# Three-sweep graph network on one core: constants in one late transfer, the input by chunks, the first band as two tiles

## The chip, the core and the metric

One core of one Trainium2 chip runs the kernel. The metric is the device time of one execution in microseconds (us), the median of several runs. The profile is one further execution of the same kernel; its "span" runs from its first to its last instruction. Engines: PE is TensorE (PEld its weight loads), DVE is VectorE, ACT is ScalarE, POOL is GpSimd, SP is SyncE, which here only issues DMAs.

## The reference

All arrays are float32. `x` is 4096 x 128, `adj` is 4096 x 4096, all weights are 128 x 128.

```python
def _mlp(x, W1, b1, W2, b2, W3, b3):
    a = jax.nn.leaky_relu
    x = a(x @ W1 + b1, NEG_SLOPE)
    x = a(x @ W2 + b2, NEG_SLOPE)
    return a(x @ W3 + b3, NEG_SLOPE)

u, v = (x, v_node_feats)
for _ in range(3):
    v = _mlp(adj @ u, uv_W1, uv_b1, uv_W2, uv_b2, uv_W3, uv_b3)
    u = _mlp(adj @ v, vu_W1, vu_b1, vu_W2, vu_b2, vu_W3, vu_b3)
y = _layernorm(x + v)
return _layernorm(y + adj @ (y @ gcn_weight))
```

## The kernel before

The work is six products with the same 4096 x 4096 matrix (five through the network, one for the last layer). The output rows are cut into 8 **chunks** of 512. The matrix comes from memory in **bands** of 1 MB, each 128 partitions by 2048 elements: one chunk of rows against one chunk of columns. A band is two **tiles** of 128 x 1024. 500 tiles are loaded in all and the list `visits` names 768 visits, since a tile may serve two sums.

To keep float32 accuracy each tile is split: ACT makes a rounded copy `high` (`split`, L442 to L446), DVE makes the rest `low` = raw - high (L568 to L570), and PE then runs three matmuls for each half of a tile (`multiply`, L777, matmuls of L790): six matmuls of 512 columns a visit. The input `x` is split in the same way, chunk by chunk, by `raise_x` (ACT, L450) and `lower_x` (DVE, L575) ahead of the first eight bands. Four of the seven weights are split by `raise_weights` (ACT, L453 to L457) and `lower_weights` (DVE, L578 to L581).

All engines follow one plan. Each runs a loop over the step n, one step for one visit, and issues what is due in that step; semaphores order the engines. In step n an engine first does what belongs to a chunk of finished sums, then its tiles. A tile's `high` is due about six visits ahead of its own visit, its `low` four ahead. Steps 0 to 15 are the first chunk of rows (bands 0 to 7, one visit for each tile). In step 16 ACT rounds the first finished sum (`raise_sum`, L471 to L473), in step 17 DVE makes its rest (`lower_sum`, L607 to L609), and in step 19 PE runs the first dense layer (`layer_1`, L719): three matmuls, L708 and L709 on the rounded sum and L711 on the rest. Before them it waits until all four weights are split. Before the change ACT and DVE split the weights in step 15 (L531 and L667): on ACT behind the split of tile 20 and ahead of that of tile 21, on DVE ahead of `low` of tile 19.

Buffers: `raw` holds 4 bands (`RAWS` = 8 tiles), `high` and `low` 8 tiles each. SP issues all bands and all of `x` on one hardware queue, in program order; band b (from 4 on) is issued when DVE has lowered both tiles of band b - 4:

```python
                if t >= RAWS:
                    sp.wait_ge(low_ready, t - RAWS + IN_BAND)
```

The input comes in four pieces of 1, 1, 2 and 4 chunks (256, 256, 512 and 1024 KB), so the queue's order before is: x piece 0, band 0, x piece 1, band 1, x piece 2, band 2, band 3, x piece 3, band 4, band 5 and so on. The 13 transfers of weights and biases (four biases of 128 x 1, seven weights and two spread biases of 128 x 128, 0.59 MB) are issued by POOL on the software queue right at the start (L427 to L431); one semaphore counts them all.

Of the kernel before, what the change touches and what calls it, by code (L numbers as in the profile page):

```python
# [12 lines left out]
D = 128  # L13
# [11 lines left out]
RAWS = 8  # L25
# [4 lines left out]
BANKS = 5  # L30
HELD = 8

X_PIECES = [1, 1, 2, 4]

OPENED = 3
SLOPE = 0.01
# [207 lines left out]
            holder[s.bank] = i  # L244

def gnn_kernel(nc, adj, x_nodes, weights, biases, spread, out):
    plan = Plan()
    tiles, visits, sums, chunks = plan.tiles, plan.visits, plan.sums, plan.chunks
    END = len(visits) + 16  # L250
# [1 line left out]
    with ExitStack() as ctx:  # L252
        def sbuf(name, shape, dtype=F32):
            return ctx.enter_context(nc.sbuf_tensor(name, shape, dtype))
# [4 lines left out]
        def sem(name):  # L259
            return ctx.enter_context(nc.semaphore(name))  # L260
# [9 lines left out]
        part = sbuf("part", [D, N - CHUNK])  # L270
        w_high = {name: sbuf(f"w_high_{name}", [D, D], F32R) for name in SPLIT}
        w_low = {name: sbuf(f"w_low_{name}", [D, D], F32R) for name in SPLIT}
        w = {name: sbuf(f"w_{name}", [D, D]) for name in WEIGHTS}
        b = {name: sbuf(f"b_{name}", [D, 1]) for name in BIASES}
        b_spread = {name: sbuf(f"b_{name}", [D, D]) for name in SPREAD}
        eps = sbuf("eps", [D, 1])
        h = [sbuf(f"h{i}", [D, CHUNK]) for i in range(2)]
        h_high = sbuf("h_high", [D, CHUNK], F32R)
# [8 lines left out]
        layer = [psum(f"layer{i}", [D, CHUNK]) for i in range(2)]  # L287
        proj = psum("proj", [D, CHUNK])

        x_loaded = [sem(f"x_loaded{i}") for i in range(len(X_PIECES))]  # L290
        consts_loaded = sem("consts_loaded")
        consts_set = sem("consts_set")
        band_loaded = [sem(f"band_loaded{s}") for s in range(RAWS // IN_BAND)]
# [30 lines left out]
        out_stored = sem("out_stored")  # L324
        last_stored = sem("last_stored")

        N_CONSTS = 16 * (len(WEIGHTS) + len(BIASES) + len(SPREAD))
        FINAL = len(chunks) - CHUNKS
        NORM = FINAL - CHUNKS

# [2 lines left out]

        def raw_of(t):
            return raw[t % RAWS // IN_BAND][:, bass.ds(t % IN_BAND * TILE, TILE)]

        def piece_of(chunk):
            return next(i for i in range(len(X_PIECES)) if chunk < sum(X_PIECES[:i + 1]))

        def block_in(tile, j):  # L340
            return tile[:, j * D:(j + 1) * D]
# [56 lines left out]

        @block.sync
        def _(sp):  # L400
            def load_x(piece):
                of_piece = bass.ds(sum(X_PIECES[:piece]) * CHUNK, X_PIECES[piece] * CHUNK)
                sp.dma_start(resid[:, of_piece], x_nodes[:, of_piece]).then_inc(x_loaded[piece], 16)

            def load(t):
                if t >= RAWS:
                    sp.wait_ge(low_ready, t - RAWS + IN_BAND)
                sp.dma_start(raw[t % RAWS // IN_BAND][:], adj[tiles[t][0], tiles[t][1] // IN_BAND]).then_inc(
                    band_loaded[t % RAWS // IN_BAND], 16)

            for t in range(0, len(tiles), IN_BAND):
                for piece in range(len(X_PIECES)):
                    if t == sum(X_PIECES[:piece]) * IN_BAND:
                        load_x(piece)
                load(t)

            for i in (len(chunks) - 2, len(chunks) - 1):
                sp.wait_ge(normed_ready, i - NORM + 1)
                sp.dma_start(out[sum_of(i).chunk], part_of(sum_of(i).chunk)).then_inc(last_stored, 16)
            sp.wait_ge(last_stored, 32)  # L420

        @block.gpsimd
        def _(pool):
            nc.gpsimd.memset(eps[:], EPS).then_inc(consts_set, 1)
            for name in BIASES:
                pool.dma_start(b[name][:], biases[name]).then_inc(consts_loaded, 16)  # L427
            for name in WEIGHTS:
                pool.dma_start(w[name][:], weights[name]).then_inc(consts_loaded, 16)
            for name in SPREAD:  # L430
                pool.dma_start(b_spread[name][:], spread[name]).then_inc(consts_loaded, 16)  # L431
            for i in range(FINAL, len(chunks) - 2):
                pool.wait_ge(normed_ready, i - NORM + 1)
                pool.dma_start(out[sum_of(i).chunk], part_of(sum_of(i).chunk)).then_inc(
                    first_stored if i == FINAL else out_stored, 16)
            pool.wait_ge(first_stored, 16)
            pool.wait_ge(out_stored, 16 * (CHUNKS - 3))
# [2 lines left out]
        @block.scalar  # L440
        def _(act):
            def split(t):  # L442
                act.wait_ge(band_loaded[t % RAWS // IN_BAND], 16 * (t // RAWS + 1))
                if t >= SLOTS:
                    act.wait_ge(visited, plan.closing[t - SLOTS] + 1)
                nc.scalar.activation(high[t % SLOTS][:], raw_of(t), ACT.Copy).then_inc(high_ready, 1)  # L446

            def raise_x(c):
                act.wait_ge(x_loaded[piece_of(c)], 16)
                nc.scalar.activation(p_high[0][:, blocks_of(c)], resid[:, blocks_of(c)],  # L450
                                     ACT.Copy).then_inc(p_high_ready, 1)

            def raise_weights():  # L453
                act.wait_ge(consts_loaded, N_CONSTS)
                act.wait_ge(consts_set, 1)
                for name in SPLIT:
                    nc.scalar.activation(w_high[name][:], w[name][:], ACT.Copy).then_inc(w_high_ready, 1)  # L457
# [70 lines left out]
                nc.scalar.activation(h[i % 2][:], acc[sum_of(i).bank][:], ACT.Copy).then_inc(taken, 1)  # L528

            for n in range(END):  # L530
                if n == TILES - 1:  # L531
                    raise_weights()
                for i, chunk in enumerate(chunks):
                    if n == chunk.start and not chunk.halves and not finishes(i):
                        take(i)
                    if layered(i):
                        if n == chunk.start and chunk.halves:
                            raise_sum(i)
                        if n == chunk.start + (LAYER_1 if chunk.halves else WHOLE_LAYER_1):
                            first_layer(i)  # L540
                        if n == chunk.start + (LAYER_2 if chunk.halves else WHOLE_LAYER_2):
                            second_layer(i)
                        if n == chunk.third + THIRD:
                            third_layer(i)
                    if normed(i):
                        if n == chunk.third + ROOT:
                            deviation(i)
                        if n == chunk.third + NORMALIZE:
                            normalize(i)
                            raise_normed(i)  # L550
                    if not layered(i):
                        if n == chunk.start + LAST_ROOT:
                            deviation(i)
                        if n == chunk.start + LAST_NORMALIZE:
                            normalize(i)
                for s in sums:
                    if s.goal == "keep" and n == s.read:
                        keep(s)
                for t in range(len(tiles)):
                    if n == split_at[t]:  # L560
                        if t % IN_BAND == 0 and t // IN_BAND < CHUNKS:
                            raise_x(t // IN_BAND)
                        split(t)
# [3 lines left out]
        def _(dve):  # L567
# [96 lines left out]
                                        ALU.subtract).then_inc(p_low_ready, 1)  # L664

            for n in range(END):
                if n == TILES - 1:  # L667
                    lower_weights()
                for i, chunk in enumerate(chunks):
                    if n == chunk.start and finishes(i):  # L670
# [170 lines left out]
```

## Time and profile before

| | |
|---|---|
| runs | 1181.62 us, median of 3 (1181.33 to 1182.02) |
| profiled execution, its own time | 1181.15 us |
| its span, first to last instruction | 1179.2 us |
| PE busy | 1154.8 us, 98% of the span |
| DVE, ACT busy | 739.8 us (63%), 680.8 us (58%) |
| read from memory | 264.8 MB, 226 GB/s over the span |

1.95 us of the profiled execution lie outside its span. The rows below come from this execution. Their times are in us from the first instruction. In a timeline row stand start, length, engine, line, operation, output<-input and shape, with the idle time before it and what ended that in brackets; "x2" means that two neighbours of a kind are merged. In a row of stretches stand the stretch, its length, the busy time of PE, PEld, DVE, ACT and POOL (with counts), the granted TensorE clock, the busy share of the DMA engines and GB/s.

### The profile page before, as it was taken

To read this page: it belongs to the slowest core of one execution; us is meant where nothing else is said; L and a number is where in the kernel's file an instruction comes from. 1 tells how busy PE (TensorE), PEld (TensorE's weight loads), DVE (VectorE), ACT (ScalarE), POOL (GpSimd) and SP (SyncE) were. 2 spreads that over 40 slices of the span, in tenths; PEclk is the share of its full clock that TensorE was granted. 3 is DMA by queue.
4 is the path that set the end of the run, shared out by engine and by line. 5 is a ranking of instruction groups with operands and counts; after the bars stand their busy time and mean duration, and the time that the engine had idled before them with its cause. 6 is when DMAs were issued, how large, how long until landed. Compare 5 with 4: busy or idle time off the path is not lost.

```text
span 1179.2 us, 13786 instructions
## 1 busy us (share of the span) xinstructions
PE 1154.8 (98%) x5216; PEld 950.7 (81%) x5216; DVE 739.8 (63%) x879; ACT 680.8 (58%) x855; POOL 10.5 (1%) x24
## 2 busy tenths in 40 slices
PE   5999999999999999999999999999999999999997
PEld 3788888888788888888888878888887888888886
DVE  5986555554845554765564484555578655669996
ACT  5876544555554444764454474544477655557784
POOL 2000000000000000000000000000000000000000
PEclk9999999999999999999999999999999999999999
DMA  8987665644834446645544574444657454458994
GB/s 351 382 317 276 230 248 214 250 160 189 306 148 186 178 185 219 261 169 193 214 183 162 209 289 176 178 178 178 250 215 266 162 185 181 185 195 342 353 347 173
DMA packets 37823, 267.82 MB, mean 227 GB/s; under 512 B 4464, under 2 KB 4464, under 8 KB 5632
## 3 DMA queue, kind: packets, MB, share of 16 engines
q1 hardware_dynamic: 36864, 264.78, 60.0%
q0 software_dynamic: 896, 2.17, 0.5%
q8 instruction: 43, 0.70, 0.2%
q14 instruction: 20, 0.16, 0.0%
HBM read 264.83 MB, written 2.10 MB: 226 GB/s over the span
## 4 chain that ended last, share of the span: by engine, by line
PE 91%; DVE 5%; DMA 3%; ACT 1%; issue 1%; ACTq 0%; SPq 0%; DVEq 0%
PE acc L790 82%; PE proj L746 3%; DVE low L570 3%; DMA raw<-adj_dram 3%; PE layer L711 1%; PE layer L708 1%; PE layer L709 1%; PE layer L740 1%; PE layer L729 1%; DVE stats L644 0%; ACT part L513 0%; DVE h L640 0%; ACT high L446 0%; DVE h L604 0%; DVE moments L647 0%
## 5 line engine op out<-in xcount | busy, mean ns | idle before, releaser
L790 PE MATMUL acc<-high,p_low 128*128 128x512 f32 x1536 | 609.3, 397 | 14.2 <-DVE low L570 14.2
L570 DVE TENSOR_TENSOR low<-raw,high 128x1024 fp32r<-128x1024 f32 x500 | 584.5, 1218 | 36.8 <-ACT high L446 36.8
L790 PE MATMUL acc<-low,p_high 128*128 128x512 f32 x1536 | 599.6, 390 | 0.0
L790 PE MATMUL acc<-high,p_high 128*128 128x512 f32 x1536 | 598.9, 390 | 0.0
L446 ACT ACTIVATE high<-raw 128x1024 fp32r<-128x1024 f32 x500 | 500.2, 1050 | 80.9 <-DMA raw<-adj_dram 40.8
L790 PEld LDWEIGHTS acc<-high,p_low 128*128 128x128 f32 x1536 | 289.1, 188 | 78.9 <-DVE low L570 17.8
L790 PEld LDWEIGHTS acc<-high,p_high 128*128 128x128 f32 x1536 | 289.1, 188 | 61.4 <-issue 2.9
L790 PEld LDWEIGHTS acc<-low,p_high 128*128 128x128 f32 x1536 | 288.9, 188 | 61.4
L473 ACT ACTIVATE h_high<-h 128x512 fp32r<-128x512 f32 x21 | 13.3, 632 | 134.1 <-DVE h L604 134.1
L604 DVE TENSOR_TENSOR h<-acc,part 128x512 f32<-128x512 f32 x36 | 24.8, 689 | 100.8 <-PE acc L790 93.2
L614 DVE TENSOR_TENSOR h_low<-h,h_high 128x512 fp32r<-128x512 f32 x32 | 22.1, 692 | 70.2 <-ACT h L483 70.2
L619 DVE TENSOR_TENSOR h<-proj,b_uv_b 128x512 f32<-128x512 f32 x24 | 16.6, 690 | 63.9 <-PE proj L746 63.9
L609 DVE TENSOR_TENSOR h_low<-acc,h_high 128x512 fp32r<-128x512 f32 x11 | 7.6, 691 | 77.8 <-ACT h_high L473 77.8
L498 ACT ACTIVATE p_high<-h 128x512 fp32r<-128x512 f32 x32 | 20.2, 632 | 48.5 <-DVE h L619 48.0
L473 ACT ACTIVATE h_high<-acc 128x512 fp32r<-128x512 f32 x11 | 6.6, 596 | 72.1 <-PE acc L790 72.1
L619 DVE TENSOR_TENSOR h<-proj,b_vu_b 128x512 f32<-128x512 f32 x16 | 11.1, 691 | 41.6 <-PE proj L746 41.6
L488 ACT ACTIVATE h<-layer,b_uv_b 128x512 f32<-128x512 f32 x24 | 16.5, 688 | 30.3 <-PE layer L711 24.3
L481 ACT ACTIVATE h_high<-layer,b_uv_b 128x512 fp32r<-128x512 f32 x20 | 13.7, 686 | 34.1 <-PE layer L711 34.1
L500 ACT ACTIVATE h<-h 128x512 f32<-128x512 f32 x40 | 24.8, 620 | 9.9 <-DVE h L619 9.8
L746 PEld LDWEIGHTS proj<-w_uv_W,h 128*128 128x128 f32 x192 | 25.1, 191 | 2.0
L463 ACT ACTIVATE part<-acc 128x512 f32<-128x512 f32 x36 | 21.4, 595 | 7.4 <-PE acc L790 7.0
L746 PE MATMUL proj<-w_uv_W,h 128*128 128x128 f32 x192 | 25.3, 275 | 0.0
(64 smaller groups left out, 379.6 us busy)
## 6 DMA issues: line engine op xcount, KB each, us to landing
raw<-adj_dram SPq DMA_DIRECT2D x250, 1024.0 KB, 4.9
out_dram<-part POOLq DMA_DIRECT2D x6, 256.0 KB, 5.1
resid<-x_dram SPq DMA_DIRECT2D x1, 1024.0 KB, 18.2
resid<-x_dram SPq DMA_DIRECT2D x2, 256.0 KB, 5.9
resid<-x_dram SPq DMA_DIRECT2D x1, 512.0 KB, 13.0
out_dram<-part SPq DMA_DIRECT2D x2, 256.0 KB, 2.0
w_uv_W<-uv_W_dram POOLq DMA_DIRECT2D x3, 64.0 KB, 7.8
w_vu_W<-vu_W_dram POOLq DMA_DIRECT2D x3, 64.0 KB, 7.9
```

The lines of the kernel that those rows point to most:

```text
L446: nc.scalar.activation(high[t % SLOTS][:], raw_of(t), ACT.Copy).then_inc(high_ready, 1)
L463: nc.scalar.activation(part_of(s.chunk), acc[s.bank][:], ACT.Copy).then_inc(part_kept, 1)
L473: nc.scalar.activation(h_high[:], summed(i)[:], ACT.Copy).then_inc(sum_raised, 1)
L488: nc.scalar.activation(h[i % 2][:], layer[1][:], ACT.Prelu, bias=b[f"{way_of(i)}_b2"][:], alpha=SLOPE).then_inc(second_ready, 1)
L498: nc.scalar.activation(p_high[k % 2][:, blocks_of(c)], h[i % 2][:], ACT.Prelu, alpha=SLOPE).then_inc(p_high_ready, 1)
L500: nc.scalar.activation(h[i % 2][:], h[i % 2][:], ACT.Prelu, alpha=SLOPE).then_inc(third_ready, 1)
L570: nc.vector.tensor_tensor(low[t % SLOTS][:], raw_of(t), high[t % SLOTS][:].bitcast(F32), ALU.subtract).then_inc(low_ready, 1)
L604: nc.vector.tensor_tensor(h[i % 2][:], acc[s.bank][:], part_of(s.chunk), ALU.add).then_inc(total_ready, 1)
L614: nc.vector.tensor_tensor(h_low[:], h[i % 2][:], h_high[:].bitcast(F32), ALU.subtract).then_inc(first_lowered, 1)
L619: nc.vector.tensor_tensor(h[i % 2][:].rearrange("p (j d) -> p j d", d=D), proj[:].rearrange("p (j d) -> p j d", d=D), b_spread[f"{way_of(i ...
L746: done = nc.tensor.matmul(block_in(proj, j), block_in(source, j), weight[:], start=True, stop=True)
L790: done = nc.tensor.matmul(bank[:], p[parity][:, at:at + D], a[slot][:, columns], start=(n == s.opens and j == 0 and m == 0), stop=(n == s. ...
```

## The change

- The 13 small transfers on POOL's queue go. One DRAM tensor holds all weights, the two spread biases and the four biases side by side (128 rows of 4624 bytes), and SP loads it in one transfer, issued after band 7 and ahead of band 8. In the chip's memory it is one tile `const`, of which the old names are slices.
- The input comes in eight chunks of 256 KB, each issued right ahead of its band (chunk k ahead of band k, k = 0 to 7), each with its own semaphore.
- Band 0 is loaded as two transfers of one tile each (rows of 4096 bytes instead of 8192), with a semaphore for the first tile.
- The weights are split in step 17 instead of step 15: on ACT behind the split of tile 22 and ahead of that of tile 23; on DVE behind `low` of tile 20, ahead of the rest of the sum and of `low` of tile 21.

The queue's order after: x chunk 0, tile 0, tile 1, x chunk 1, band 1, ..., x chunk 7, band 7, constants, band 8, band 9 and so on.

```diff
-X_PIECES = [1, 1, 2, 4]
+CONSTS_BEHIND = TILES
...
-        w = {name: sbuf(f"w_{name}", [D, D]) for name in WEIGHTS}
-        b = {name: sbuf(f"b_{name}", [D, 1]) for name in BIASES}
-        b_spread = {name: sbuf(f"b_{name}", [D, D]) for name in SPREAD}
+        const = sbuf("const", [D, (len(WEIGHTS) + len(SPREAD)) * D + len(BIASES)])
+        w = {name: const[:, bass.ds(i * D, D)] for i, name in enumerate(WEIGHTS)}
+        b_spread = {name: const[:, bass.ds((len(WEIGHTS) + i) * D, D)] for i, name in enumerate(SPREAD)}
+        b = {name: const[:, bass.ds((len(WEIGHTS) + len(SPREAD)) * D + i, 1)] for i, name in enumerate(BIASES)}
...
-            def load_x(piece):
-                of_piece = bass.ds(sum(X_PIECES[:piece]) * CHUNK, X_PIECES[piece] * CHUNK)
-                sp.dma_start(resid[:, of_piece], x_nodes[:, of_piece]).then_inc(x_loaded[piece], 16)
+            def load_x(c):
+                sp.dma_start(resid[:, blocks_of(c)], x_nodes[:, blocks_of(c)]).then_inc(x_loaded[c], 16)
 
             def load(t):
+                if t == 0:
+                    sp.dma_start(raw_of(0), adj[tiles[0][0], 0, :, 0:TILE]).then_inc(first_loaded, 16)
+                    sp.dma_start(raw_of(1), adj[tiles[0][0], 0, :, TILE:]).then_inc(band_loaded[0], 16)
+                    return
...
             for t in range(0, len(tiles), IN_BAND):
-                for piece in range(len(X_PIECES)):
-                    if t == sum(X_PIECES[:piece]) * IN_BAND:
-                        load_x(piece)
+                if t == CONSTS_BEHIND:
+                    sp.dma_start(const[:], consts).then_inc(consts_loaded, 16)
+                if t // IN_BAND < CHUNKS:
+                    load_x(t // IN_BAND)
                 load(t)
...
             nc.gpsimd.memset(eps[:], EPS).then_inc(consts_set, 1)
-            for name in BIASES:
-                pool.dma_start(b[name][:], biases[name]).then_inc(consts_loaded, 16)
-            for name in WEIGHTS:
-                pool.dma_start(w[name][:], weights[name]).then_inc(consts_loaded, 16)
-            for name in SPREAD:
-                pool.dma_start(b_spread[name][:], spread[name]).then_inc(consts_loaded, 16)
...
             def split(t):
-                act.wait_ge(band_loaded[t % RAWS // IN_BAND], 16 * (t // RAWS + 1))
+                if t == 0:
+                    act.wait_ge(first_loaded, 16)
+                else:
+                    act.wait_ge(band_loaded[t % RAWS // IN_BAND], 16 * (t // RAWS + 1))
...
             def raise_weights():
-                act.wait_ge(consts_loaded, N_CONSTS)
+                act.wait_ge(consts_loaded, 16)
...
             for n in range(END):
-                if n == TILES - 1:
+                if n == TILES + 1:
                     raise_weights()
...
             for n in range(END):
-                if n == TILES - 1:
+                if n == TILES + 1:
                     lower_weights()
```

## Rows read from the trace of the kernel before

**Rows 1.** The page: busy time of PE, and PE in 40 slices of the span.
```profile
PE 1154.8 (98%) x5216; PEld 950.7 (81%) x5216; DVE 739.8 (63%) x879; ACT 680.8 (58%) x855; POOL 10.5 (1%) x24
...
PE   5999999999999999999999999999999999999997
```

**Rows 2.** Stretches of the opening, and the last store of 256 KB (last row).
```profile
2.00:3.50 1.50, 0.00 (x0) 0.00 (x0) 0.00 (x0) 0.02 (x1) 1.50 (x3) 1.00 0.85 201
...
6.00:7.50 1.50, 0.00 (x0) 0.00 (x0) 0.00 (x0) 0.00 (x0) 1.50 (x4) 1.00 0.35 116
...
16.00:26.00 10.00, 8.60 (x36) 6.51 (x36) 7.43 (x8) 5.82 (x8) 0.00 (x0) 1.00 1.02 424
...
1177.65:1178.35 0.70, 0.00 (x0) 0.00 (x0) 0.00 (x0) 0.00 (x0) 0.00 (x0) 0.50 0.96 366
```

**Rows 3.** PE's waits from 0 to 60: us in total, times, longest us.
```profile
PE acc L790 <- DVE low L570: 13.4, 4, 10.0
```

**Rows 4.** Timeline of PE, from its first matmul to the first dense layer.
```profile
9.97 0.79 PE L790 MATMUL acc<-high,p_low 128*128 128x512 f32 x1 [9.97 <-DVE low L570]
...
10.99 0.63 PE L790 MATMUL acc<-low,p_high 128*128 128x512 f32 x1
...
11.42 0.63 PE L790 MATMUL acc<-high,p_low 128*128 128x512 f32 x1
...
27.88 0.50 PE L790 MATMUL acc<-high,p_low 128*128 128x512 f32 x1 [1.57 <-DVE low L570]
...
43.82 0.47 PE L708 MATMUL layer<-h_high,w_low_uv_W 128*128 128x512 f32 x1 [0.22 <-ACT h_high L473]
...
45.51 0.50 PE L711 MATMUL layer<-h_low,w_high_uv_W 128*128 128x512 f32 x1 [0.98 <-DVE h_low L609]
```

**Rows 5.** The chain of waits from 0 to 60: start, us, what.
```profile
34.74 5.63 DMA raw<-adj_dram
...
46.01 4.08 PE acc L790 x18
```

**Rows 6.** Timeline of ACT in the opening.
```profile
4.16 0.63 ACT L450 ACTIVATE p_high<-resid 128x512 fp32r<-128x512 f32 x1 [2.15 <-DMA resid<-x_dram]
7.61 2.00 ACT L446 ACTIVATE high<-raw 128x1024 fp32r<-128x1024 f32 x2 [2.81 <-DMA raw<-adj_dram]
9.98 0.63 ACT L450 ACTIVATE p_high<-resid 128x512 fp32r<-128x512 f32 x1 [0.37 <-DMA resid<-x_dram]
13.54 2.01 ACT L446 ACTIVATE high<-raw 128x1024 fp32r<-128x1024 f32 x2 [2.94 <-DMA raw<-adj_dram]
...
18.05 2.00 ACT L446 ACTIVATE high<-raw 128x1024 fp32r<-128x1024 f32 x2 [1.86 <-DMA raw<-adj_dram]
...
37.91 2.01 ACT L446 ACTIVATE high<-raw 128x1024 fp32r<-128x1024 f32 x2 [0.46 <-DMA raw<-adj_dram]
40.39 1.06 ACT L446 ACTIVATE high<-raw 128x1024 fp32r<-128x1024 f32 x1 [0.47 <-DMA raw<-adj_dram]
41.36 0.49 ACT L457 ACTIVATE w_high_uv_W<-w_uv_W 128x128 fp32r<-128x128 f32 x2
41.75 0.49 ACT L457 ACTIVATE w_high_vu_W<-w_vu_W 128x128 fp32r<-128x128 f32 x2
```

**Rows 7.** Timeline of DVE around the first dense layer.
```profile
42.09 0.48 DVE L581 TENSOR_TENSOR w_low_vu_W<-w_vu_W,w_high_vu_W 128x128 fp32r<-128x128 f32 x2
42.50 2.35 DVE L570 TENSOR_TENSOR low<-raw,high 128x1024 fp32r<-128x1024 f32 x2
44.77 0.68 DVE L609 TENSOR_TENSOR h_low<-acc,h_high 128x512 fp32r<-128x512 f32 x1
```

**Rows 8.** DMA queues from 5.5 to 8: the software queue's packets, MB, share.
```profile
q0 software_dynamic: 52, 0.00, 1.6%
```

**Rows 9.** Two stretches behind PE's last matmul.
```profile
1172.50:1176.50 4.00, 0.00 (x0) 0.00 (x0) 2.16 (x11) 1.67 (x5) 0.00 (x0) 1.00 0.00 0
1176.70:1179.00 2.30, 0.00 (x0) 0.00 (x0) 0.00 (x0) 0.07 (x1) 0.00 (x0) 0.50 0.30 114
```

More of the change, by code:

```diff
@@ L244, in place_banks, with gnn_kernel @@
             holder[s.bank] = i
-def gnn_kernel(nc, adj, x_nodes, weights, biases, spread, out):
+def gnn_kernel(nc, adj, x_nodes, consts, out):
     plan = Plan()
@@ L288, in gnn_kernel @@
         proj = psum("proj", [D, CHUNK])
-        x_loaded = [sem(f"x_loaded{i}") for i in range(len(X_PIECES))]
+        x_loaded = [sem(f"x_loaded{c}") for c in range(CHUNKS)]
+        first_loaded = sem("first_loaded")
         consts_loaded = sem("consts_loaded")
@@ L325, in gnn_kernel @@
         last_stored = sem("last_stored")
-        N_CONSTS = 16 * (len(WEIGHTS) + len(BIASES) + len(SPREAD))
         FINAL = len(chunks) - CHUNKS
@@ L335, in raw_of @@
             return raw[t % RAWS // IN_BAND][:, bass.ds(t % IN_BAND * TILE, TILE)]
-        def piece_of(chunk):
-            return next(i for i in range(len(X_PIECES)) if chunk < sum(X_PIECES[:i + 1]))
         def block_in(tile, j):
@@ L448, in raise_x @@
             def raise_x(c):
-                act.wait_ge(x_loaded[piece_of(c)], 16)
+                act.wait_ge(x_loaded[c], 16)
                 nc.scalar.activation(p_high[0][:, blocks_of(c)], resid[:, blocks_of(c)],
@@ L831 @@
     x_nodes = put("x_dram", _np.asarray(inputs["x"]).reshape(N // D, D, D).transpose(1, 0, 2).reshape(D, N))
-    weights = {k: put(f"{k}_dram", inputs[v]) for k, v in _WEIGHTS.items()}
-    biases = {k: put(f"{k}_dram", _np.asarray(inputs[v]).reshape(D, 1)) for k, v in _BIASES.items()}
-    spread = {k: put(f"{k}_dram", _np.broadcast_to(_np.asarray(inputs[v]).reshape(1, D), (D, D)))
-              for k, v in _SPREAD.items()}
+    consts = put("const_dram", _np.concatenate(
+        [_np.asarray(inputs[_WEIGHTS[k]]) for k in WEIGHTS]
+        + [_np.broadcast_to(_np.asarray(inputs[_SPREAD[k]]).reshape(1, D), (D, D)) for k in SPREAD]
+        + [_np.asarray(inputs[_BIASES[k]]).reshape(D, 1) for k in BIASES], axis=1))
     out = nc.dram_tensor("out_dram", (CHUNKS, D, CHUNK), F32, kind="ExternalOutput").ap()
-    gnn_kernel(nc, adj, x_nodes, weights, biases, spread, out)
+    gnn_kernel(nc, adj, x_nodes, consts, out)
     r = _run(nc, [arrays], core_ids=[0])
```

## The prediction

> **What bounds the kernel now.** I read the page first: PE is busy for 98% of the span, and of 40 slices only the first is half empty [rows 1]. So PE's work sets the time, and an edit that leaves that work alone can only win in the opening. The last slice (7) is the tail behind the last sum, which the change doesn't touch. Next, PE's waits of the first 60 us: 13.4 us on `low`, of which 10.0 are the start and 3.4 three later waits [rows 3]. The timeline gives the rest: 1.57 us ahead of 27.88, then 0.22 and 0.98 us at the first dense layer [rows 4]. Behind 46.01 the chain of waits is PE's own matmuls [rows 5]. Whatever the change brings must therefore show as an earlier start of L711, the last matmul of that layer, which is at 45.51 now. Behind it PE never catches up with its inputs in this stretch, so a shift there should pass one for one to the end.
>
> What holds up L711? The stretch from 16 to 26 has DMA engines at a share of 1.02 and 424 GB/s [rows 2], ACT waits for landings over and over [rows 6], and the chain has band 10 landing at 34.74 + 5.63 = 40.37 [rows 5]. In the opening the DMA queue is the bound, not PE. Two bands land 2.48 us apart when the queue is full, 37.91 to 40.39 [rows 6].
>
> **How full the queue is before.** From band 0 (7.59) to band 10 (40.37) pass 32.78 us. The transfers in between, at full rate: ten bands, 10 x 2.48 = 24.80; x piece 1, 0.70 (price below); pieces 2 and 3, 1.57 MB at 424 GB/s, 3.71; weights and biases, 0.59 MB, 1.39. Sum 30.60. So **2.18 us are lost**, and the rows show where: from 6.0 to 7.5 the share falls to 0.35 and the rate to 116 GB/s [rows 2], while POOL's queue moves 52 packets that sum to 0.00 MB [rows 8]. x piece 1 lands at 9.98, 2.37 us behind band 0 [rows 6]. I read this as the biases, rows of 4 bytes, holding up every DMA engine in turn. From band 2 (18.05) on I see no loss.
>
> **The change, part by part.**
>
> *Constants in one transfer behind band 7.* It removes POOL's 13 issues (hidden before: nobody waits for POOL's engine, only for the weights' landing, and that was long past by 41) and the 2.18 us of loss. The bytes themselves are not saved: 1.39 us, only later in the queue, yet ahead of band 8 and so of band 11. Rows of 4624 bytes lie between rows that I have at full rate.
>
> *Input by chunks.* Until band 7 the same bytes have passed as before. Rows are 2048 bytes for all seven later chunks. No clean load of that kind is in the trace; the nearest row is the last store of 256 KB with such rows: it fits into 0.70 us at 366 GB/s [rows 2]. The other end is chunk 0 itself at 201 GB/s [rows 2], 1.30 us, but there the queue is just starting. I take 0.70, since the store runs on a warm queue as chunks 1 to 7 will: 7 x 0.70 = 4.90 against 0.70 + 3.71 = 4.41 before, a cost of 0.49. Four more issues on SP pass while the queue holds earlier transfers, so they cost nothing; with an empty queue each would push back the band behind it by its own length.
>
> *Band 0 as two tiles.* The first tile should land near 6.2, about half way from chunk 0 (4.16) to 7.59 and a little more, and PE then starts 2.38 us later (7.61 to 9.97) [rows 4, 6], at 8.6 instead of 9.97. The second may come 0.1 later than band 0 did (double the rows): 7.69. The bounds of that are 0 and, at chunk 0's rate, 1 MB at 201 GB/s against 424, 2.7. I count **nothing for the early start**: chunk plus band is 3.18 us, PE needs 2.73 a band at full clock, so PE is soon waiting for the queue again, with gaps of 0.4 us a band. It does bring the clock up a little sooner (matmuls are 0.43 us apart at 11 us, which is 1.2 GHz for 512 columns, and 0.227 apart in the chain's 18 [rows 4, 5]; the clock column reads 1.00 even before PE's first matmul, so at the start I go by the spacing), and that too is swallowed. A band is 12 matmuls, hence the 2.73.
>
> *Weights split in step 17.* This moves more than it seems. Eight small instructions are issued behind the split of tile 22, so they wait for **band 11**, where they waited for band 10. On the other side DVE no longer has two `low` (2.27 us, from 42.50 to 44.77) between the weights and the rest of the sum [rows 7]. From the landing of the band to L711: before 45.51 - 40.37 = 5.14. After: 0.02, then `high` 0.97 (40.39 to 41.36), four roundings 0.88 (41.36 to 42.24), 0.02, the last `low` of a weight 0.21, the sum's rest 0.68, issue 0.06 [rows 6, 7], in all 2.84. The next two `low` come behind, for visits 21 and 22, 2.7 us away: covered. So the step costs one band and gives back 2.30: a net cost of 0.18.
>
> **The sum.** Second tile 7.69; seven chunks 4.90; eleven bands 27.28; constants 1.39: band 11 lands at 41.26 (before: 40.37 + 2.48 = 42.85). Plus 2.84 is L711 at 44.10 against 45.51: **1.4 us earlier**. Term by term: 2.18 - 0.49 - 0.10 - 0.18 = 1.41. PE is not the limit there: band 8 lands at 33.82, PE opens it at 36.2 and is through visit 18 at 40.3. Against its own time, 1181.15, the profiled execution would come to 1179.7; it lay 0.47 under the median, and against the median of the runs I predict **1180.2**. I expect the raw buffers not to interfere: band 11 may be issued when tile 15 is lowered, near 33.2, and the queue is then still at band 8.
>
> What a measurement can tell from no change is about 0.2%, 2.4 us. The forecast lies inside that.
>
> **Rivals.**
>
> *A. Band 0's slow start goes too.* Band 0 took 7.59 - 4.16 = 3.43 us where 2.48 is the full rate. If POOL's descriptors were the cause, 0.95 more is saved: 1179.2. Against: the software queue's packets show up only in the window from 5.5 on [rows 8], when band 0 is nearly through.
>
> *B. The loss stays.* If the hole at 6 to 7.5 belongs to the start of the hardware queue and not to the biases, 2.18 us come back and the moved step still costs: 1182.4, slower. For it: chunk 0 was slow before any bias moved. Against: the hole begins just when those packets do.
>
> *C. The clock falls in the new wait.* PE is done with visit 18 at 40.3 and the weights are ready at 43.44, so two short waits (0.22 and 0.98) become one of 3.1 us. In the trace a wait of 1.57 us and the two at the dense layer left the matmuls at 0.227 apart [rows 4, 5]; behind the last matmul the granted clock stood at 1.00 over a stretch of 4 us and was 0.50 from 1176.7 [rows 9]. The new wait lies between. Price, by the start: about 13 matmuls at 0.43 instead of 0.23, 2.6 us, all behind the last wait on the queue and so not hidden: 1182.8, slower by 1.2. It decides as soon as the fall comes at all. The Trainium skill, TensorE: Matmul & The Clock Gate (the part on the clock gate), says that the throttled state is the default and activity lifts it, which is what both rows show; it doesn't say that a wait of this size does no harm.
>
> *D. Small rows are slow every time.* If each of the seven chunks runs at chunk 0's 201 GB/s, 0.60 more each: 4.2, so 1184.4, slower. It decides from 0.90 us a chunk. Against it: the store row. The Trainium skill, DMA: Bandwidth & Descriptors (section Rules for kernel authors), asks for at least 1 MiB a transfer, and its fit of 2.0 us plus the bytes would make a chunk 2.6 us if nothing overlapped, an estimate that would end near 1193.5. The trace speaks against reading it so: bands of 1 MB follow each other at 424 GB/s, with no fixed part between them [rows 2].
>
> *E. The split of band 0 is what counts.* An early start worth 1.4 us would only add if PE and not the queue were the bound up to 45; the 1.02 share denies it. No chance of its own.
>
> **How the numbers follow.** Forecast 0.61, A 0.15, B 0.09, C 0.09, D 0.06. The predicted time is the forecast's. Faster by over 0.2% means below 1179.3: half of A and the forecast's lower tail, 0.18. Slower by over 0.2% means above 1184.0: D and a clock that falls for longer, 0.08. Between them 0.74. The range goes from just under A (1178.8) to just over C (1183.0); D and the tails of A are left out.
>
> **What would show it.** Right: POOL has no DMA; x chunk 1 lands 0.7 to 0.8 behind the second tile, and the share stays near 1.0 from 6 to 33; PE starts near 8.6 and still has gaps of 0.3 to 0.5 us ahead of bands 3 to 7; the constants land near 31.3 and band 11 near 41.3; L708 waits some 3.1 us for `low` of the weights; L711 starts near 44.1 and the granted clock stays at 1.00. Wrong: chunks that take over 0.9 us (D); a hole in DMA share without POOL's packets (B); matmuls 0.43 apart behind L711 (C); or a time that drops by clearly more than L711 moves, which would mean that something behind 46 us changed and that I missed it.

## The result, and the profile after

| | runs | median, us |
|---|---|---|
| before | 8 | 1181.38 (1180.15 to 1182.02) |
| after | 8 | 1184.61 (1183.75 to 1185.83) |

The ratio is 1.0023, with a 95% interval from 1.0015 to 1.0032: slower by 2.7 us (the two medians lie 3.2 apart), where 1.4 us faster was forecast. The profiled execution took 1184.88 us (before 1181.15), its span 1182.9 us (before 1179.2), 3.7 us more.

The page of the kernel after answers to [rows 1]: POOL's 13 issues are gone, the first slice is fuller, and PE's busy time is 4.5 us larger with the same count of matmuls. This is the first sign that PE itself has become slower.

```profile
PE 1159.3 (98%) x5216; PEld 951.4 (80%) x5216; DVE 740.6 (63%) x879; ACT 680.9 (58%) x855; POOL 3.7 (0%) x11
...
PE   6899999999999999999999999999999999999997
```

**The opening** came out nearly as forecast. ACT's timeline of the kernel after, as in [rows 6]:

```profile
6.76 1.06 ACT L446 ACTIVATE high<-raw 128x1024 fp32r<-128x1024 f32 x1 [2.55 <-DMA raw<-adj_dram]
8.01 1.06 ACT L446 ACTIVATE high<-raw 128x1024 fp32r<-128x1024 f32 x1 [0.19 <-DMA raw<-adj_dram]
...
23.75 2.01 ACT L446 ACTIVATE high<-raw 128x1024 fp32r<-128x1024 f32 x2 [0.63 <-DMA raw<-adj_dram]
...
26.91 2.01 ACT L446 ACTIVATE high<-raw 128x1024 fp32r<-128x1024 f32 x2 [0.63 <-DMA raw<-adj_dram]
...
38.97 2.01 ACT L446 ACTIVATE high<-raw 128x1024 fp32r<-128x1024 f32 x2 [0.47 <-DMA raw<-adj_dram]
...
41.45 1.06 ACT L446 ACTIVATE high<-raw 128x1024 fp32r<-128x1024 f32 x1
42.41 0.49 ACT L457 ACTIVATE w_high_uv_W<-const 128x128 fp32r<-128x128 f32 x2
```

Chunk plus band come every 3.16 us (23.75 to 26.91), band 10 lands at 38.94 (in the chain, 30.40 + 8.55) and band 11 about 2.48 later, near 41.42.

**The first dense layer.** PE's timeline of the kernel after; [rows 4] has the same lines of before:

```profile
43.69 0.50 PE L708 MATMUL layer<-h_high,w_low_uv_W 128*128 128x512 f32 x1 [2.95 <-DVE w_low_vu_W L581]
44.03 0.39 PE L709 MATMUL layer<-h_high,w_high_uv_W 128*128 128x512 f32 x1
44.29 0.75 PE L711 MATMUL layer<-h_low,w_high_uv_W 128*128 128x512 f32 x1
44.84 0.63 PE L790 MATMUL acc<-high,p_low 128*128 128x512 f32 x1
45.27 0.63 PE L790 MATMUL acc<-high,p_high 128*128 128x512 f32 x1
...
47.40 0.57 PE L790 MATMUL acc<-high,p_low 128*128 128x512 f32 x1
47.81 0.39 PE L790 MATMUL acc<-high,p_high 128*128 128x512 f32 x1
48.04 0.40 PE L790 MATMUL acc<-low,p_high 128*128 128x512 f32 x1
```

L711 starts at 44.29, 1.22 us earlier than before. Then the matmuls are 0.43 apart instead of 0.227. The stretches (columns as in [rows 2]) show the granted clock at half:

```profile
40.00:44.30 4.30, 1.35 (x7) 0.59 (x5) 2.79 (x7) 4.25 (x9) 0.00 (x0) 1.00 1.01 417
44.40:47.70 3.30, 3.30 (x9) 2.62 (x9) 3.30 (x4) 2.73 (x4) 0.00 (x0) 0.50 0.64 206
47.80:52.00 4.20, 4.20 (x20) 3.42 (x19) 4.20 (x5) 3.01 (x5) 0.00 (x0) 1.00 0.98 406
```

From 44.29 to 47.81 pass 3.52 us for eight matmuls; at 0.227 they take 1.82. So the fall costs 1.70 us: more than the opening had won.

**The rest of the kernel.** A shift of a PE-bound kernel should stay as it is. It does not. Here are eight matmuls of the third dense layer of one early and one late chunk of rows, for before and then for after:

```profile
108.36 1.05 PE L746 MATMUL proj<-w_uv_W,h 128*128 128x128 f32 x8
...
1032.48 1.05 PE L746 MATMUL proj<-w_uv_W,h 128*128 128x128 f32 x8
```

```profile
108.98 1.05 PE L746 MATMUL proj<-const,h 128*128 128x128 f32 x8
...
1035.61 1.05 PE L746 MATMUL proj<-const,h 128*128 128x128 f32 x8
```

Between the same two places pass 924.12 us before and 926.63 after: **2.51 us of drift**. PE has one wait between them, of 1.4 us for `h_high`, and it is the same in both; the granted clock is 1.00 throughout in both. The source of the drift is small and repeated. Behind a dense layer, from L708 to the 13th matmul from there, before (first fence) takes 2.74 us and after (second) 2.79:

```profile
70.60 0.40 PE L708 MATMUL layer<-h_high,w_low_uv_W 128*128 128x512 f32 x1
...
73.34 0.39 PE L790 MATMUL acc<-high,p_low 128*128 128x512 f32 x1
```

```profile
71.04 0.40 PE L708 MATMUL layer<-h_high,w_low_uv_W 128*128 128x512 f32 x1
71.27 0.40 PE L709 MATMUL layer<-h_high,w_high_uv_W 128*128 128x512 f32 x1
71.51 0.39 PE L711 MATMUL layer<-h_low,w_high_uv_W 128*128 128x512 f32 x1
...
73.83 0.39 PE L790 MATMUL acc<-high,p_low 128*128 128x512 f32 x1
```

The median distance is 0.227 us for nearly all matmuls of both kernels. Behind a dense layer before has five longer ones, 0.231 to 0.234, and is then back at 0.227; after has 0.231 to 0.237 for eleven of the first thirteen. Between the two places lie 56 dense layers of this form, which makes 2.51 some 0.045 us for each. Compared matmul by matmul, 2.3 of the 2.51 us arise in the first fifteen distances behind such a layer.

The ledger of the 3.7 us, after less before: L711 -1.22; clock +1.70; so +0.48, and +0.44 is seen at 70.6 (71.04 less 70.60). Up to 108 the rows say +0.62, then 2.51 of drift, +3.13 at 1032, and 0.5 more in what is left. In the last stage PE is not always ahead of DVE: it waits for `low` again, here the rows of before (1100 to 1172) and of the last kernel below, which differs from before in the opening alone:

```profile
PE acc L790 <- DVE low L570: 0.8, 2, 0.4
```

```profile
PE acc L788 <- DVE low L568: 2.0, 3, 1.0
```

In after they are 1.1 us. Over all profiles of this document they lie between 0.5 and 2.6 us, and the stretch from the place at 1032 to PE's last matmul between 139.2 and 141.8. So differences of under 2 us between two profiles' ends show nothing by themselves, and an earlier start of L711 can be lost there in part.

### The profile page after: what moved, and what is told of

Its sections match the earlier page's. It is cut to its first block, busy times and chain, and to the rows that moved or that the text cites. A ratio compares the mean times of both kernels' runs of the same rounds, so it can differ in the third digit from the quotient of the medians.

```text
span 1182.9 us, 13779 instructions
## 1 busy us (share of the span) xinstructions
PE 1159.3 (98%) x5216; PEld 951.4 (80%) x5216; DVE 740.6 (63%) x879; ACT 680.9 (58%) x855; POOL 3.7 (0%) x11
## 3 DMA queue, kind: packets, MB, share of 16 engines
q0 software_dynamic: 480, 1.57, 0.3%
## 4 chain that ended last, share of the span: by engine, by line
PE 89%; DVE 5%; DMA 4%; ACT 1%; issue 1%; SPq 0%; ACTq 0%; DVEq 0%
PE acc L790 81%; DMA raw<-adj_dram 4%; PE proj L746 3%; DVE low L570 3%; PE layer L708 1%; PE layer L711 1%; PE layer L709 1%; PE layer L740 1%; PE layer L729 1%; DVE stats L644 1%; ACT part L513 0%; DVE h L640 0%; ACT high L446 0%; DVE h L604 0%; DVE moments L647 0%
## 5 line engine op out<-in xcount | busy, mean ns | idle before, releaser
L446 ACT ACTIVATE high<-raw 128x1024 fp32r<-128x1024 f32 x500 | 500.3, 1050 | 78.8 <-DMA raw<-adj_dram 39.7
L619 DVE TENSOR_TENSOR h<-proj,const 128x512 f32<-128x512 f32 x40 | 27.6, 690 | 109.4 <-PE proj L746 109.4
L488 ACT ACTIVATE h<-layer,const 128x512 f32<-128x512 f32 x40 | 27.5, 688 | 54.9 <-PE layer L711 43.0
L481 ACT ACTIVATE h_high<-layer,const 128x512 fp32r<-128x512 f32 x32 | 22.0, 686 | 59.5 <-PE layer L711 59.5
L746 PEld LDWEIGHTS proj<-const,h 128*128 128x128 f32 x384 | 50.0, 191 | 5.2 <-ACT h L528 1.1
L746 PE MATMUL proj<-const,h 128*128 128x128 f32 x384 | 50.8, 275 | 0.7 <-ACT h L528 0.7
L483 ACT ACTIVATE h<-layer,const 128x512 f32<-128x512 f32 x40 | 27.2, 681 | 5.5 <-PE layer L729 5.5
```

What stands on the lines that cost most here:

```text
L481: nc.scalar.activation(h_high[:], layer[0][:], ACT.Prelu, bias=bias, alpha=SLOPE).then_inc(first_raised, 1)
L483: nc.scalar.activation(h[i % 2][:], layer[0][:], ACT.Prelu, bias=bias, alpha=SLOPE).then_inc(first_ready, 1)
L488: nc.scalar.activation(h[i % 2][:], layer[1][:], ACT.Prelu, bias=b[f"{way_of(i)}_b2"][:], alpha=SLOPE).then_inc(second_ready, 1)
L619: nc.vector.tensor_tensor(h[i % 2][:].rearrange("p (j d) -> p j d", d=D), proj[:].rearrange("p (j d) -> p j d", d=D), b_spread[f"{way_of(i ...
L746: done = nc.tensor.matmul(block_in(proj, j), block_in(source, j), weight[:], start=True, stop=True)
```

## The experiments

Each comparison has its own runs of the kernel before beside it. "Drift" is the distance between the two places above, less 924.12. A kernel that ran once has one time, and is read here for its trace. Two profiles of kernels with the same opening also differ in it: band 10 landed between 39.7 and 40.7 in the five kernels that load as before does, between 38.7 and 40.0 in the nine that load as after does, and at 37.4 and 37.5 in the two with the constants alone. A difference in the opening of less than about 1 us between two profiles is not shown.

### What causes the drift: the data, the order, or the place of the tiles?

**Old addresses, everything else as after:**

```diff
+        pad = sbuf("pad", [D, 24])
         eps = sbuf("eps", [D, 1])
```

> The changed kernel with 96 unused bytes a partition behind the constants' tile, so that h, h_high, h_low and the small tiles lie where they lay before the change. Theory A (the drift comes from these tiles' addresses, 96 bytes lower since the biases no longer have padding): matmuls behind each dense layer go back from 231 to 236 ns apart to 227, the drift between 92 us and the end falls from 3.1 us to under 0.3, and the time falls by some 3 us to about 1181.6. Theory B (semaphore numbers) and theory C (the constants as slices of one tile, or the way they are loaded): drift unchanged at 3.1 us, time 1184.6. The fall of the clock near 45 us stays in either.

1182.92 us (10 runs, 1180.51 to 1183.98), ratio 1.0005 [0.9994, 1.0015]. The drift is gone:

```profile
109.62 1.05 PE L747 MATMUL proj<-const,h 128*128 128x128 f32 x8
...
1033.74 1.05 PE L747 MATMUL proj<-const,h 128*128 128x128 f32 x8
```

924.12, as before. The time is 1.2 over before's beside it (1181.72) and 1.3 over what I expected. The wait and the fall were in that expectation; what differs in this profile is that the opening itself ran later than after's (L708 at 44.71, after 43.69), so that the kernel is 1.26 us behind before at 109.62 and still 1.26 at 1033.74. The stretch behind the first dense layer reads

```profile
44.70:48.00 3.30, 3.29 (x8) 2.61 (x9) 3.30 (x4) 3.17 (x5) 0.00 (x0) 0.50 0.55 161
```

**The converse: the kernel before with only the tile's layout changed.** All 13 transfers stay on POOL; they fill slices of one tile.

```diff
-        w = {name: sbuf(f"w_{name}", [D, D]) for name in WEIGHTS}
-        b = {name: sbuf(f"b_{name}", [D, 1]) for name in BIASES}
+        const = sbuf("const", [D, (len(WEIGHTS) + len(SPREAD)) * D + len(BIASES)])
+        w = {name: const[:, bass.ds(i * D, D)] for i, name in enumerate(WEIGHTS)}
...
```

> The kernel before with one alteration: weights and biases are slices of one tile, still loaded by POOL in 13 transfers; this puts h, h_high and h_low at the changed kernel's addresses, 96 bytes lower. Theory A (addresses) and C (slices of one tile): matmuls behind dense layers at 231 to 236 ns, the end 3.1 us later against the visit at 92 us, time about 1184.5 where the kernel before has 1181.4. Theory B (semaphore numbers) and a cause in how the constants are loaded: no drift, 1181.4.

1183.96 us (10 runs, 1183.11 to 1187.48), ratio 1.0023 [1.0014, 1.0033]: the layout by itself brings the same ratio as the whole change. Drift 2.51:

```profile
107.95 1.05 PE L747 MATMUL proj<-const,h 128*128 128x128 f32 x8
...
1034.58 1.05 PE L747 MATMUL proj<-const,h 128*128 128x128 f32 x8
```

**Old semaphore numbers** (after, with the new semaphores allocated last):

> The changed kernel with the five new semaphores allocated last, so that all others have their old numbers; addresses as changed. Theory B (numbers matter): the drift between 92 us and the end falls from 3.1 us to under 0.3, matmuls behind dense layers at 227 ns. Theories A and C: drift unchanged at 3.1 us.

Drift 2.49, 1185.41 us in its one run: the semaphores' numbers are nothing.

**Which tile, and which place?** Three variants of after, with a pad of 8 or of 16 elements (32, 64 bytes) ahead of `eps`, and with 24 elements between `h` and `h_high`:

> The changed kernel with 32 unused bytes a partition behind the constants' tile: h, h_high and h_low begin 32 bytes past a multiple of 64, as before the change, but at other addresses than then (64 lower). Theory A1 (what counts is the place within 64 bytes): no drift between 92 us and the end (under 0.8 us with the noise of the last stage), matmuls behind dense layers at 227 ns. Theory A2 (another property of the old addresses counts): drift 3.1 us as in the changed kernel.

> The changed kernel with 64 unused bytes behind the constants' tile: h, h_high and h_low on multiples of 64 (and 128). Theory A1 (place within 64 bytes): drift 3.1 us, as in the changed kernel, whose tiles are on multiples of 64 too. Theory A2: may have none.

> The changed kernel with the 96 bytes between h and h_high: h (two buffers, written by ACT and DVE, read by PE in the third layer) at the changed addresses, h_high and h_low (PE's moving operands in the first two layers) at the old ones. If h_high and h_low carry the effect: no drift, and L708 to L709 at 234 to 235 ns as before. If h carries it: drift 3.1 us. If both do: something between.

And three of before: 8 elements ahead of `h_high` (so `h_low` moves too), ahead of `h_low`, and ahead of and behind `h_high`:

> The kernel before with 32 unused bytes a partition between h and h_high: h_high, h_low and the small tiles begin on a multiple of 64 (64 past a multiple of 128, as in the changed kernel), h stays. If the place of h_high and h_low makes the drift: 2.5 to 3.1 us more between 92 us and the end, time near 1184.3, L708 to L709 at 237 ns and not 234. If it takes another property: no drift.

> The kernel before with 32 unused bytes between h_high and h_low: only h_low (and the small tiles behind it) begins on a multiple of 64. If h_low's place alone makes the drift: between the visits at 92 and 1056 us the kernel falls back by 0.7 to 2.7 us, as the run with both moved did (0.74), and L710 to L712 (L709 to L711 of before) is over 232 ns. If h_high's place makes it: no drift.

> The kernel before with 32 unused bytes before and behind h_high: h_high begins on a multiple of 64, h_low 64 bytes on from its old place, again 32 past a multiple of 64. If h_high's place makes the drift: 0.7 to 2.7 us between 92 and 1056 us. If h_low's does: none.

| kernel | `h_high` starts | `h_low`, bytes past a multiple of 64 | drift, us | one time |
|---|---|---|---|---|
| before | 32 past | 32 | 0 | |
| after | on it | 0 | 2.51 | |
| after + 96 bytes | 32 past | 32 | 0.00 | |
| after + 32 | 32 past | 32 | 0.02 | 1182.63 |
| after + 64 | on it | 0 | 1.16 | 1182.91 |
| after, 96 bytes behind `h` | 32 past | 32 | -0.09 | 1184.03 |
| before, `h_high` and behind + 32 | on it | 0 | 0.70 | 1182.89 |
| before, `h_high` + 32, behind + 64 | on it | 32 | 1.10 | 1182.71 |
| before, `h_low` and behind + 32 | 32 past | 0 | 1.44 | 1183.55 |

All four kernels of the table with both tiles 32 past a multiple of 64 are free of the drift; all five with one or both on it have 0.7 to 2.5 us. `h` moved alone does nothing. The rule held each time, but its sizes don't add up (both tiles moved in before: 0.70, either one: 1.10 and 1.44; both on a multiple: 2.51, 1.16 and 0.70 in three kernels), so the mechanism stays open, and the place within 64 bytes can't be all of it. The small tiles behind `h_low` moved with it in every kernel that has `h_low` on the multiple, but the trace of the last kernel of the table has no instruction on any of them before 898.9 us, and most of its drift is there by then. The Trainium skill, SBUF — State Buffer (section Operand start alignment), asks only that an operand start at a multiple of its element's size, and says that this is about legality, not speed; all the starts here satisfy it.

### The wait at the first dense layer

**Weights split in step 15 again, the rest as after.** It takes away the one long wait, at the price that the chain goes as before.

```diff
-                if n == TILES + 1:
+                if n == TILES - 1:
                     raise_weights()
```

> The changed kernel with the weights split in step 15 again (ACT behind tile 20, DVE ahead of low of tile 19); all else as changed. Theory 1 (the long wait at the first dense layer lets the clock fall): PE's wait at L708 and L711 shrinks from 2.9 us to under 1.5, no stretch near 45 to 50 has a granted clock under 1.00, and L711 starts near 44. Against the changed kernel 1 to 1.5 us are won, so near 1183.3. Theory 2 (a drift of some 0.09 us a chunk behind the opening, whatever its cause, is the larger part of the loss): the drift stays, the last visit ends 2.8 to 3.0 us further behind than the visit at 92 us does, and the kernel stays slower than the one before by 1.5 to 2 us. If the clock were all, this kernel would come out at 1180 or below.

1183.11 us (10 runs, 1182.46 to 1186.77), ratio 1.0017 [1.0005, 1.0029]. PE's waits of its first 60 us: two in place of one.

```profile
PE layer L708 <- ACT h_high L473: 1.7, 1, 1.7
PE layer L711 <- DVE h_low L609: 1.0, 1, 1.0
```

In this profile the clock stayed up, L711 stood at 44.54, and the drift was 2.52, as it must with after's addresses. L711 stands 0.25 us later than with step 17 (44.29), which is less than two profiles of one opening differ by, so what the step is worth at L711 is not shown. What it brings is the long wait: with step 17 all six profiles have it and the fall, with step 15 and the input by chunks none of three.

**Both remedies, step 15 and the 96 bytes:**

> The changed kernel with both repairs: 96 unused bytes (old addresses) and the weights split in step 15. Theory: no drift, no fall of the clock, L711 near 44.5 as in the run with step 15 (its visit 19 was 0.95 us ahead of the kernel before). So 0.8 to 1.2 us faster than the kernel before, near 1180.6, if nothing else in the change costs; the transfers of the opening then give what the prediction hoped for, less what step 15 wins or loses against 17.

1181.96 us (11 runs, 1180.02 to 1185.18), ratio 1.0001 [0.9992, 1.0010]: no gain, and 1.4 us over what I expected, though its profile has no drift, no fall, and L711 at 44.38, 1.13 us earlier than before. The runs spread with the clock: three of mean clock 0.998 or 0.999 below 1181 and one at 1181.36, the seven of 0.996 or 0.997 from 1181.39 to 1185.18. The mean doesn't say where a clock fell. That waits of this size can bring it down is seen in the traces of the constants alone, below, and of two variants of before: with `h_low` moved the clock fell behind a wait of 1.86 us, and with `h_high` and `h_low` moved behind one of 1.88 us:

```profile
20.13 0.50 PE L791 MATMUL acc<-high,p_low 128*128 128x512 f32 x1 [1.88 <-DVE low L571]
...
20.80 0.63 PE L791 MATMUL acc<-low,p_high 128*128 128x512 f32 x1
21.22 0.63 PE L791 MATMUL acc<-high,p_low 128*128 128x512 f32 x1
```

**So: weights split ahead of the first sum.** ACT rounds them in step 12, DVE makes the rests in step 14 (the constants have landed at 31.5), with the 96 bytes:

```diff
-                if n == TILES + 1:
+                if n == TILES - 4:
                     raise_weights()
...
-                if n == TILES + 1:
+                if n == TILES - 2:
                     lower_weights()
```

> The changed kernel with 96 unused bytes (old addresses) and the weights split earlier and in different steps: ACT rounds them in step 12 (behind tile 17, so behind band 8), DVE makes the rests in step 14 (ahead of low of tile 18). Theory: the dense layer then waits for nothing but band 10's tile 20; L711 starts near 42.4, 3.1 us ahead of the kernel before and 1.7 ahead of the version with step 15; PE's wait between visit 18 and L708 shrinks to about 0.7 us, so the clock stays up in all runs. Time near 1178.8 against 1181.9 before, clearly faster. Rival: PE's idle time only moves and the clock falls in some runs all the same: then the median is near 1180.5.

1179.76 us (11 runs, 1178.46 to 1180.86; before beside it 1182.27), ratio 0.9971 [0.9958, 0.9984]: the first version that beats before, by 0.3%, and every run has a mean clock of 0.998 or 0.999. It is 1 us short of what I expected, though L711 stands where I put it (42.31, 3.20 ahead of before): 2.38 of the 3.20 are left at 60, and 1.0 at PE's last matmul in this profile. The wait ahead of L708 is down to half a microsecond:

```profile
41.59 0.47 PE L709 MATMUL layer<-h_high,w_low_uv_W 128*128 128x512 f32 x1 [0.50 <-ACT h_high L474]
```

### What the parts of the opening are worth

**The constants alone** (before, with one constant transfer behind band 7 and the 96 bytes; `x` in its old pieces, band 0 whole, split in step 15):

```diff
+                if t == TILES:
+                    sp.dma_start(const[:], consts).then_inc(consts_loaded, 16)
                 load(t)
...
-            for name in BIASES:
-                pool.dma_start(b[name][:], biases[name]).then_inc(consts_loaded, 16)
...
```

> Of the change only the constants: one tile, one transfer on SP's queue behind band 7; the input in its old four pieces, band 0 whole, weights split in step 15, 96 unused bytes (old addresses). If POOL's 13 transfers made the loss of 2.18 us: no stretch with a DMA share near 0.35 behind band 0, x piece 1 lands 0.7 to 1.0 us behind band 0, band 10 lands near 38.3 (before 40.37), L711 near 43.4. If the loss belongs to the start of the hardware queue: x piece 1 again 2.4 us behind band 0, band 10 near 40.4, L711 near 45.5.

1180.45 us in its one run. The hole of [rows 2] from 6.0 to 7.5 (share 0.35, 116 GB/s) is filled, and band 10 lands at 37.36, 3.01 us earlier than before (before: 40.37, forecast for this part: 2.18; over all profiles of either kind the difference is 2.2 to 3.3):

```profile
6.00:7.50 1.50, 0.00 (x0) 0.00 (x0) 0.00 (x0) 0.78 (x1) 0.00 (x0) 1.00 1.11 449
42.60:45.90 3.30, 3.30 (x8) 2.62 (x9) 3.30 (x4) 2.37 (x4) 0.00 (x0) 0.50 0.94 362
```

```profile
37.38 1.06 ACT L444 ACTIVATE high<-raw 128x1024 fp32r<-128x1024 f32 x1 [0.48 <-DMA raw<-adj_dram]
```

Band 0 lands at 6.70 instead of 7.58: 0.88 of the 3.01 are what rival A foretold, and the 2.13 left are the forecast's 2.18. And the second row shows the clock at half from 42.6 on, behind waits of 1.63 and 0.98 us, which it had survived in other profiles.

**Band 0 whole again** (after with both remedies, less the split of band 0):

> Both repairs (old addresses, step 15) and the constants and the input as changed, but band 0 whole again. Theory (the early start of PE is swallowed by the queue): PE starts 1 to 1.4 us later, near 9.8, and L711 and all visits from 19 on are where they are with two tiles, within 0.3 us. Rival (an early start counts): all is 1 us later.

1181.00 us in its one run. PE starts at 10.12 instead of 8.39, yet L711 is at 44.29 (with the split: 44.38). The early start of 1.7 us leaves no trace at L711, as forecast. ACT starts on band 0 at 7.75 here, without POOL's transfers, against 6.72 and 6.80 with the constants alone and 7.61 before; so taking POOL's transfers away doesn't by itself bring band 0 forward.

**The constants alone, split early** (steps 12 and 14):

> Only the constants changed (one tile, one transfer on SP behind band 7, old addresses kept by 96 unused bytes), the input in its old four pieces, band 0 whole; weights rounded in step 12 and lowered in step 14. Theory: this keeps what the changed kernel wins (POOL's transfers gone) and leaves out the rest; band 10 lands between 37.4 and 38.5, L711 starts 1.3 us or so behind PE's last wait on band 10, near 41 to 42, against 42.4 in the version with chunks. Time 1178.3 to 1179.5, no slower than the version with chunks. Rival: the input by chunks or the early start is needed to keep the clock up through the first bands; then the clock falls in more runs here and the median is above 1180.5.

1178.21 us (6 runs, 1176.81 to 1179.05; before beside it 1182.24), ratio **0.9965** [0.9953, 0.9978]. It is the simplest version, without the chunks and the split band, and its interval lies below before; against the version with chunks (0.9971) it can't be told apart. From the landing of band 10 to L711 pass 3.36 us here (37.51 to 40.87), against 5.14 before and in the version above: some 1.8 us at L711 come from the early split alone. Before has its weights by 16.2, so it could split them early too. No run has the early split on the kernel before, and how much of the 0.35% it gives without any new transfer is untested. Its granted clock behind the dense layer:

```profile
42.60:45.90 3.30, 3.30 (x15) 2.33 (x13) 1.62 (x2) 2.24 (x4) 0.00 (x0) 1.00 1.01 402
```

## Why the prediction was wrong

**What held.** The working of the opening, term by term:

| step | forecast | measured |
|---|---|---|
| second tile of band 0 lands | 7.69 | 7.98 |
| PE starts | 8.6 | 9.13 |
| chunk plus band | 3.18 | 3.16 |
| constants land | 31.3 | 31.5 |
| band 11 lands | 41.26 | 41.42 |
| wait ahead of L708 | 3.1 | 2.95 |
| L711 starts | 44.10 | 44.29 |

So B and D are out, and one pair of profiles bears out E's price of nothing. Two errors of my sum cancel, and that is luck. The constants alone bring band 10 forward by 3.01 us, where I had 2.18: they bring band 0 forward by 0.88 as well, as rival A had it. The change keeps 1.43 of that (40.37 to 38.94). I had put what the chunks and the split band cost at 0.59 (0.49 + 0.10), and here it is 1.6. The chunks behind band 0 are not the reason: from the second tile (7.98) to band 10 pass 30.96 us, from band 0 to band 10 with the constants alone 30.66, which is 0.30 for what I had at 0.49. It is the landing of band 0, 1.28 later than with the constants alone, where I had 0.10 without a row for it; with band 0 whole and the chunks kept it was 1.03 later in the one profile, so the second transfer isn't the reason either, and why band 0 lands later ahead of chunks stays open. L711 within 0.2 of the forecast is partly luck too: in the six profiles of kernels with the same opening it lies between 44.04 and 45.73.

**The step that failed.** "Behind it PE never catches up with its inputs in this stretch, so a shift there should pass one for one to the end." The change does something to PE that I costed at nothing: its new layout. I read "one tile `const`, of which the old names are slices" as bookkeeping, and followed its bytes on the queue, never the addresses of what is allocated behind it. It costs 2.5 us between 108 and 1032 in both directions of the test (layout changed alone: 2.51, old addresses restored: 0.00). The other half of the sentence, that a shift passes one for one to the end, holds from 60 to 1100 us and not outside: the last kernel above is 4.6 us ahead of before at L711, 3.6 at 60 and at 1100, and 2.1 at PE's last matmul, since PE waits for its inputs again behind L711 and in the last stage. My list of clues named a time that drops by clearly more than L711 moves, so something changed behind 46 us. I thought of it only as a gain, gave it no chance, and ended the range at 1183.0.

**Rival C was the case, at a chance of 0.09.** The wait of 2.9 us came with a fall of the clock in all six profiles that have it (after, and its variants with pads and with the old semaphores, all with step 17). Its price was 1.70 us, not 2.6: eight slow matmuls, not the 13 of the start. The chance was too low: my rows had a harmless wait of 1.57, and behind the last matmul a clock that held for some 4 us of idleness and then fell; the new wait lay between the two, and nothing in the rows spoke for one chance in eleven. The two missed causes add: 1.70 + 2.5 less 1.22 is 3.0 of the 3.7 us.

**Still open:** how the start of `h_high` and `h_low` reaches the pace of the matmuls behind the dense layer; why a wait of 1.9 us brings the clock down in two profiles and waits of 1.65 and 0.98 leave it up in others; and why the waits of the last stage differ from profile to profile.

## What to carry to other kernels

Merging, padding or reordering tiles moves all that is allocated behind them: work out the starts of the tiles that PE reads before and after, and where a PE-bound kernel changes pace with no new wait, put the old addresses back with a pad before looking further. Price a wait of PE by what the clock does behind it as well as by its length; a gain of one or two us on a queue is lost again by one wait of two or three, so move the work that PE waits for (here eight small splits) ahead into slack as soon as its data are there. Small transfers on another queue can cost a full queue more than their bytes; take them out first, and alone, since no run here shows a gain from the rest of this change.

## What the runs showed of the hardware

- Two operand tiles that start on a multiple of 64 bytes instead of 32 past one keep the matmuls behind the dense layers 0.231 to 0.237 us apart for eleven of thirteen distances, where five of them were over 0.227: 0.7 to 2.5 us in 924, with no new wait in the trace and the granted clock at 1.00. Why is open.
- The granted clock fell at the wait of 2.9 us (2.89 to 2.95) in all six profiles that have it, behind a single wait of 1.88 and one of 1.86 us, and behind 1.63 and 0.98 with two matmuls between (in one profile; in three others with 1.65 and 0.98 it stayed up). It stayed up behind 1.57 [rows 4] and 1.53. The fall at the first dense layer cost 1.7 us.
- Thirteen transfers on POOL's queue, four of them of 128 rows of 4 bytes, cost the full hardware queue 3.0 us beyond the 0.59 MB that they carry: band 10 lands that much earlier when the same bytes come in one transfer (2.2 to 3.3 over the profiles here). Whether it is the four with tiny rows or all thirteen is not shown: the hole in the share lies where the profile has only tiny packets on the software queue [rows 8], and no run takes those four away alone.
